# Additive attention: six of sixteen relus move to GpSimd, in pairs around its split

## The reference, cut to what matters

```
q = einsum('bnc,ac->bna', X, Wq);  k = einsum('bnc,ac->bna', X, Wk);  Vy = X @ Wy_w.T + Wy_b
e = relu(signed_sqrt(q[:, :, None, :] + k[:, None, :, :]))
scores = einsum('bija,a->bij', e, Wphi)
ex = exp(scores - max_j(scores));  denom = sum_j(ex)
Ew = einsum('bij,bija->bia', ex, e)
out = (einsum('bij,bjc->bic', ex, Vy) + Ew @ We_w.T + We_b * denom) / (denom + EPS_DEN)
```

## Time and profile before

| quantity | value |
|---|---|
| median of 3 runs | 6389.82 us (6387.81 to 6393.55) |
| profiled execution | 6392.27 us, span 6390.6 us |
| TensorE busy | 76% |
| VectorE busy | 72% |
| ScalarE busy | 63% |
| GpSimd busy | 24% |
| mean granted TensorE clock | 0.921 |

### The profile page before, as it was taken

The page is one execution under the profiler, slowest core; times in us unless marked ns, Lnnn a source line. Parts: engine busy times, 40 slices in busy tenths (PEclk is TensorE's granted clock), DMA queues, the critical chain, the costliest instruction groups (busy, mean ns, idle before and its releaser), DMA issues. The chain is left out here.

```text
span 6390.6 us, 74432 instructions
## 1 busy us (share of the span) xinstructions
PE 4886.3 (76%) x24108; PEld 2316.8 (36%) x24426; DVE 4620.4 (72%) x7027; ACT 4005.7 (63%) x2670; POOL 1540.2 (24%) x947
## 2 busy tenths in 40 slices
PE   5776867579964777777777777777777777749999
PEld 2332323357731222222222222222222222237777
DVE  2857658343335999999999999999999999942221
ACT  1011110210027999999999999999999999734443
POOL 1423424001001222222222222222222222213333
PEclk9988989789977999999999999999999999979999
DMA  1000000000011000000000000000000000020000
GB/s 74 0 0 0 0 0 0 31 3 10 10 67 38 2 3 2 3 2 13 3 2 3 2 15 2 2 3 2 3 9 4 2 2 4 3 79 14 13 13 7
DMA packets 37157, 70.97 MB, mean 11 GB/s; under 512 B 4576, under 2 KB 22080, under 8 KB 34240
## 3 DMA queue, kind: packets, MB, share of 16 engines
q1 hardware_dynamic: 34880, 62.53, 2.8%
q0 software_dynamic: 2176, 7.34, 0.3%
HBM read 49.94 MB, written 19.92 MB: 11 GB/s over the span
## 5 line engine op out<-in xcount | busy, mean ns | idle before, releaser
L732 DVE CUSTOM_DVE_ANT_0 e_slots<-e_slots,banks 128x1024 f32<-128x1024 f32 x2048 | 2418.6, 1216 | 219.5 <-PE banks L510 213.7
L572 ACT ACTIVATE e_slots<-e_slots,eps_rho 128x4096 f32<-128x4096 f32 x512 | 1885.7, 3707 | 17.7
L510 PE MATMUL banks<-ex_parts,sel 128*128 128x512 bf16 x3778 | 1216.6, 400 | 677.8 <-DVE ew L732 586.7
L467 PE MATMUL banks<-e_slots,w_score 128*32 128x512 f32 x8192 | 1158.6, 653 | 121.6 <-ACT e_slots L572 96.0
L563 ACT ACTIVATE e_slots<-k,qt 128x1024 f32<-128x1024 f32 x1024 | 1107.8, 1136 | 101.7 <-DVE ew L732 97.5
L510 PEld LDWEIGHTS banks<-ex_parts,sel 128*128 128x128 bf16 x4096 | 276.3, 100 | 1572.0 <-DVE ew L732 1329.0
L624 POOL TENSOR_SCALAR part<-ex,masks 128x1024 bf16<-128x1024 f32 x128 | 143.1, 1118 | 2745.5 <-ACT ex L579 1470.1
L689 DVE TENSOR_SCALAR e_slots<-k,qt 128x1024 f32<-128x1024 f32 x1024 | 753.3, 777 | 6.1 <-DVE den L703 6.0
L1546 PE MATMUL banks<-g_h,r_h 128*128 128x512 f32 x1024 | 410.4, 401 | 0.9 <-POOL g_l L1666 0.9
L476 PE MATMUL banks<-sel 128*128 128x256 bf16 x2304 | 406.2, 288 | 0.1
L1546 PE MATMUL banks<-g_l,r_h 128*128 128x512 f32 x1024 | 404.4, 395 | 0.0
(11 more groups left out here) (257 smaller groups left out, 6617.0 us busy)
## 6 DMA issues: line engine op xcount, KB each, us to landing
stage<-in_h SPq DMA_DIRECT2D x8, 1024.0 KB, 4.9
x_tokens<-in_x SPq DMA_DIRECT2D x1, 4096.0 KB, 17.8
w_down<-in_w_down SPq DMA_DIRECT2D x1, 4096.0 KB, 13.0
x_between<-x_tokens SPq DMA_DIRECT2D x8, 512.0 KB, 3.1
kx<-x_between SPq DMA_DIRECT2D x8, 512.0 KB, 4.7
v_all<-v_out POOLq DMA_DIRECT2D x8, 512.0 KB, 3.2
vy<-v_all SPq DMA_DIRECT2D x4, 1024.0 KB, 5.2
xg<-x_between SPq DMA_DIRECT2D x32, 128.0 KB, 2.5
```

Of the source, the lines that this page charges most:

```text
L467: ins = nc.tensor.matmul(banks[REP * COLG * g:REP * COLG * (g + 1), half, :], c_["w_score"][:, s, :], e_slots[:, par, COLG * s + g, half * ...
L510: ins = nc.tensor.matmul(spread[n % 2][:, half * W:(half + 1) * W], c_["sel"][:, n, :], ex_parts[:, par, half * W:(half + 1) * W], start=T ...
L572: nc.scalar.activation(e_slots[:, par, four, :], e_slots[:, par, four, :], ACT.Sqrt, bias=eps_rho[:, 0:1]).then_inc(sqrt_done, 1)
L732: nc.vector.tensor_tensor_reduce(out=e, in0=e, in1=spread[n % 2], scale=1.0, scalar=0.0, op0=ALU.mult, op1=ALU.add, accum_out=ew[:, q, pla ...
```

## The change

Z_BY becomes `PPPPAAAAAPPVVVVV`: GpSimd (P) makes the relus of places 0 to 3, 9 and 10, ScalarE those of 4 to 8, VectorE those of 11 to 15. GpSimd makes one as two instructions, max(min(k2, FLT_MAX), -q) and then (+ q) * 1.0, which is relu(k + q); it takes two places at a time (`two_z`), so that the second instruction of a place doesn't follow its first directly. Pairs (0, 1) and (2, 3) stand before the split of a tile, pair (9, 10) behind it. For this the queries are kept negated too (`q_pairs` and `qt` have one more dimension). The roots wait for a third semaphore, `z_p`, where places of GpSimd are among their four. ScalarE's list becomes: exponential, relus 5, 6, 7, table load, root 0, relu 8, roots 1, 2, 3, relu 4 of t+3, table load. VectorE makes relus 11 and 12 behind place 14, and 13, 14, 15 behind place 15. The group's end goes to places 2, 3, 14 and 15, behind the relus there. Scores are spread one piece per place, with m = 0 at place 15 of the tile before, and `keep_clock` has six places instead of eight.

```
-    Z_BY = "VVAAAAAAAAVVVVVV"
-    Z_AFTER = {1: [0], 2: [1], 14: [10, 11], 15: [12, 13, 14, 15]}
-    EXT_AT, MAX_AT, END_AT = 1, 6, 2
-    SCORES_AHEAD = {11: [0], 13: [1]}
-    SCORES_AT = {1: [2, 3], 2: [4], 3: [5], 4: [6], 5: [7]}
-    IDLE_AT, IDLE_PRODUCTS = (6, 7, 8, 9, 10, 12, 14, 15), 3
+    Z_BY = "PPPPAAAAAPPVVVVV"
+    Z_AFTER = {14: [11, 12], 15: [13, 14, 15]}
+    EXT_AT, MAX_AT, END_AT = 1, 6, {2: 0, 3: 1, 14: 2, 15: 3}
+    SCORES_AHEAD = {15: [0]}
+    SCORES_AT = {0: [1], 1: [2], 2: [3], 3: [4], 4: [5], 5: [6], 6: [7]}
+    IDLE_AT, IDLE_PRODUCTS = (8, 9, 10, 11, 12, 13), 3
+    FLT_MAX = 3.4028234663852886e38
...
# ScalarE
-            def first_root(t, par, freed):
-                for n in (2, 3):
-                    relu(t, par, n, freed)
-                sqrt(t, par, 0)
-            def other_roots(t, par, freed):
-                for n in (4, 5, 6, 7):
-                    relu(t, par, n, freed)
+            def before_exp(t, par, freed):
+                relu(t, par, 4, freed)
+            def behind_exp(t, par, freed):
+                for n in (5, 6, 7):
+                    relu(t, par, n, freed)
                 nc.scalar.preload_act_table(ACT.Sqrt)
-                sqrt(t, par, 1)
-                for n in (8, 9):
-                    relu(t, par, n, freed)
-                sqrt(t, par, 2)
-                sqrt(t, par, 3)
+                sqrt(t, par, 0)
+                relu(t, par, 8, freed)
+                for s in (1, 2, 3):
+                    sqrt(t, par, s)
...
# GpSimd
+            def two_z(t, par, two, freed):
+                count = Z_BY.count("P")
+                for i, n in enumerate(two):
+                    pool.wait_ge(qt_ready, t + 1)
+                    if freed is not None:
+                        pool.wait_ge(xb_freed, freed + (n + 3))
+                    pool.sem_inc(z_begun, 1)
+                    nc.gpsimd.tensor_scalar(e_slots[:, par, n, :], k2[:, :], FLT_MAX,
+                                            qt[:, par, 1, place(n):place(n) + 1], ALU.min, ALU.max).then_inc(z_clamped, 1)
+                for i, n in enumerate(two):
+                    e = e_slots[:, par, n, :]
+                    pool.wait_ge(z_clamped, t * count + z_count("P", n + 1))
+                    pool.sem_inc(z_begun, 1)
+                    nc.gpsimd.tensor_scalar(e, e, qt[:, par, 0, place(n):place(n) + 1], 1.0,
+                                            ALU.add, ALU.mult).then_inc(z_p, 1)
+            def step(t, par, last=False):
+                if not last:
+                    two_z(t + 2, par, (0, 1), t * NP)
+                    two_z(t + 2, par, (2, 3), t * NP)
+                pool.wait_ge(bc_done, t * NP)
+                parts(t + 1, 1 - par)
+                if not last:
+                    two_z(t + 2, par, (9, 10), t * NP)
...
# VectorE, at a new batch and in a tile
+                    dve.wait_ge(z_p, b * (NTI * Z_BY.count("P")))
-                nc.vector.tensor_copy(q_pairs[:, :], c_["q_next"][:, :]).then_inc(kq_taken, 1)
+                nc.vector.tensor_copy(q_pairs[:, 0, :], c_["q_next"][:, :])
+                nc.vector.tensor_scalar(q_pairs[:, 1, :], c_["q_next"][:, :], -1.0, None, ALU.mult).then_inc(kq_taken, 1)
-                    if ends is not None and END_AT <= n < END_AT + 4:
-                        group_end(ends, n - END_AT)
                     if queries is not None:
                         for m in Z_AFTER.get(n, ()):
                             z(t + 2, par, m, t * NP)
+                    if ends is not None and n in END_AT:
+                        group_end(ends, END_AT[n])
```

More of the change, by code:

```diff
@@ L195, in adaln_kernel @@
                      + LN_BUFFERS("k"))
-        c_ = phase([("e_slots", [P, 2, NP, T], fp32), ("k2", [P, T], fp32), ("q_pairs", [P, T // 2], fp32),
+        c_ = phase([("e_slots", [P, 2, NP, T], fp32), ("k2", [P, T], fp32), ("q_pairs", [P, 2, T // 2], fp32),
                     ("k2_next", [P, T], fp32), ("q_next", [P, T // 2], fp32), ("vy", [P, JT, C], fp32),
-                    ("xg", [P, CC, P], fp32), ("qt", [P, 2, NP], fp32), ("ex", [P, T], fp32),
+                    ("xg", [P, CC, P], fp32), ("qt", [P, 2, 2, NP], fp32), ("ex", [P, T], fp32),
                     ("part", [P, T], bf16), ("ex_parts", [P, 2, T], bf16), ("ex_t", [P, JT, GT, TI], fp32),
@@ L563, in relu @@
                 nc.scalar.activation(e_slots[:, par, n, :], k2[:, :], ACT.Relu,
-                                     bias=qt[:, par, place(n):place(n) + 1]).then_inc(z_a, 1)
+                                     bias=qt[:, par, 0, place(n):place(n) + 1]).then_inc(z_a, 1)
             def sqrt(t, par, s):
                 four = slice(COLG * s, COLG * (s + 1))
-                for who, sem_ in (("V", z_v), ("A", z_a)):
+                for who, sem_ in (("V", z_v), ("A", z_a), ("P", z_p)):
                     if who in Z_BY[four]:
@@ L632, in parts @@
                                         ALU.subtract).then_inc(parts_done, 1)
+            def two_z(t, par, two, freed):
+                count = Z_BY.count("P")
+                for i, n in enumerate(two):
+                    assert Z_BY[n] == "P"
+                    pool.wait_ge(qt_ready, t + 1)
[10 more added lines that the diff above has]
+                                            ALU.add, ALU.mult).then_inc(z_p, 1)
             pool.wait_ge(c_loaded, 16 * N_C_LOADS)
+            for par in range(2):
+                for two in ((0, 1), (2, 3), (9, 10)):
+                    two_z(par, par, two, None)
             parts(0, 0)
-            parts(1, 1)
-            with pool.Fori(1, TILES // 2) as u:
-                for par in range(2):
-                    pool.wait_ge(bc_done, u * (2 * NP) + (par - 1) * NP)
-                    parts(u * 2 + par, par)
+            def step(t, par, last=False):
[6 more added lines that the diff above has]
+                    two_z(t + 2, par, (9, 10), t * NP)
+            step(0, 0)
+            step(1, 1)
+            with pool.Fori(1, TILES // 2 - 1) as u:
+                step(u * 2, 0)
+                step(u * 2 + 1, 1)
+            step(TILES - 2, 0, True)
             end_phase(pool, ph["C"])
@@ L688, in z @@
                 dve.wait_ge(qt_ready, t + 1)
[L689 removed]
+                nc.vector.tensor_scalar(e_slots[:, par, n, :], k2[:, :], qt[:, par, 0, place(n):place(n) + 1], 0.0,
                                         ALU.add, ALU.max).then_inc(z_v, 1)
```

23 lines of the change are left out of this document (11 added, 12 removed).

## The result

| quantity | before | after |
|---|---|---|
| median (range) | 6388.8 us (6381.9 to 6393.6) | 6461.7 us (6458.1 to 6462.1) |
| ratio to before | | 1.0114, 95% interval 1.0096 to 1.0131 |
| span of the profiled execution | 6390.6 us | 6456.2 us |
| VectorE, ScalarE, GpSimd, TensorE busy | 72, 63, 24, 76% | 71, 55, 52, 75% |
| mean granted TensorE clock | 0.921 | 0.924 |

The change makes the kernel 73 us slower. The forecast was 6244 us, between 6130 and 6430; sign and range are both wrong.

A forecast was written before the change was run, and what follows sets the result against it. VectorE and ScalarE were taken to be at their limit, GpSimd idle for three quarters. Four tiles at 25.4 plus 5.2 us make 106.8 against 111.4, 146 us less over 127 tiles: 6244 us, range 6130 to 6430.

The forecast's parts named there:

- Prices of the new work: GpSimd's twelve new instructions per tile at 1.12 us each; with its split of 6.9 us, 20.1 us per tile.
- rival 2: GpSimd becomes the bound: 6360 us at 1.33 us an instruction, 7406 us at 2.14; chance 0.16.
- The collision: VectorE's five relus meet GpSimd's last pair and cost 2.25 us per tile, between 0.9 and 4.5.
- Turns: VectorE's relus and GpSimd's last pair alternate, relus waiting 0.25, 1.0 and 1.0 us: 2.25 us per tile; chance 0.50.
- rival 1: GpSimd keeps the port for its pair (6384 us) or VectorE for its burst (6250 to 6345); chance 0.24.
- rival 3: No collision worth naming, relus falling behind GpSimd's last pair; tiles of 24.8 us on ScalarE's loop, 6110 us; chance 0.10.
- ScalarE's wait: ScalarE waits 1.1 us per tile for the row maximum, making its loop 24.8 us.
- Small ones: Negated queries, added waits for GpSimd at the seam, six relus saved on ScalarE, TensorE's shifted scores and fillers: said to cancel.
- the clock: TensorE's shifted work cost nothing; a low clock in every tile would add 1.0 us per tile; chance 0.04.
- The group's end: VectorE's extra work per four tiles: 3.4 us plus 1.8 of meetings with GpSimd, 5.2 us, between 3.4 and 7.

The follow-up runs named there:

- e1: The kernel after with 52 satisfied waits ahead of phase C on VectorE, so its loop code lies 26 instructions later; 6337.7 us.
- e8: e1 with GpSimd's last pair (9, 10) 2 columns wide instead of 1024, so the output isn't the reference's; 6110.1 us.
- e9: e1 with six more idle TensorE products, whose result isn't used, at place 1; 6304.7 us.
- e4: The kernel before with only the group's end moved to places 2, 3, 14 and 15, where after has it; 6379.5 us.
- e11: e1 with the group's end back at places 2 to 5, as before the change; 6328.2 us.

## Why the prediction was wrong

**Prices of the new work: right.** GpSimd's instructions take 1.11 us free of a collision, as from the earlier trace rows; their means of 1176 and 1186 ns hold the meetings with VectorE. GpSimd isn't the bound (rival 2), and ScalarE waits for it ahead of a root only once, 6.9 us. (In rival 2 the 6360 us take in the group's end and the 7406 do not; nothing hangs on it.)

**The collision: right in kind, nearly in size.** Turns, 2.25 us forecast, 1.9 measured. Neither side goes through its burst while the other waits (rival 1). The shortest groups of e1 have their four tiles in 107 us (27.3, 25.9, 27.0 and 26.8), forecast 106.8. And rival 3's conditions, made real in e8, give 102.4 for four tiles and 6110 us; the prediction had 102.6 and 6110 for them. Part of this is luck. The shortest tile of e1 lasts 25.9 us, not 25.4, and what comes on top of four such is 3.4 us, not 5.2: misses of 2.0 and 1.8 us that cancel. For a kernel without falls and stops the sum was close: 127 tiles at 107.0 / 4 would be an estimated 154 us less than before's phase, forecast 146.

**ScalarE's wait: too small, and harmless.** 1.8 us a tile (224.8 / 124) for the maximum, 1.1 forecast. ScalarE isn't the bound, as it waits for VectorE's slots besides (418 us).

**"Small ones" is the step that failed,** with two terms.

The larger one isn't in the sum at all: the code. I counted instructions by their durations only, and took it for granted that an engine has its next instruction at hand. The profile of before held the sign, the row of stops ahead of the copy of the queries (4.4 us, 8 times) and 68 packets of instructions, and I passed over both. After had its loop 11 instructions earlier and 24 shorter, which put it over a block's border: 75 us of stops and, with the falls of the clock behind them (in 85 tiles instead of 53), 124 us in all (after against e1).

The other term is the clock, costed at nothing because TensorE "waits for VectorE before most spreads", with "+1.0 us per tile" as a risk that took 0.04 of the chance. At places 3 to 6 it is the other way round: there a piece of the scores stands ahead of each spread, and VectorE waits for TensorE, 0.6 us in a tile at full clock and 2.1 with a fall. The falls were there before the change and cost plain tiles nothing; now a tile with one mostly lasts 1.5 to 2.0 us longer. In e1 the splits go from 2006.9 to 5489.6 us: 27.42 us per tile, 0.55 less than before and not 1.15, where tiles without falls would give 1.2. That is why the shifted kernel gains 53 us (by the profiled executions 65) and not 146. The scores did double, as written (1.06 to 1.94 us), but the wait is VectorE's for the spreads behind them and not ScalarE's for the maximum, 1.7 us in either stretch. What makes one group fall and its neighbour not, I can't say; e9 shows only that work for TensorE at place 1 wins 33 us of it back.

**The group's end** was costed at 5.2 us, a collision of its parts at 1.8 of them; the tiles show 3.4. e4 and e11 show no more than 0.3% for its place in either direction; that part of the change neither helps nor explains the loss.

## What to carry to other kernels

Before a difference of 1 or 2% is put down to an edit of a long unrolled loop, look for idle time named "issue" at the loop's head and for packets on the instruction queue, and run a control in which only the code is moved by some satisfied waits. Price the work of an engine that takes turns with another by where in the tile it lies: six relus a tile on GpSimd are worth 53 us with the last pair beside VectorE's relus and 229 us with all pairs beside its reductions. And ask of each longer stretch of one engine what TensorE does in it: its clock is paid for in the tiles behind, once the engine that waits for it has lost its slack.

## What the runs showed of the hardware that was new to me

- A loop on VectorE of 281 or 305 instructions is fetched anew in each pass or not, by its place alone; the engine then stands still 0.3 to 3.7 us per pass in the mean, until 1.7 to 2.3 us after a packet of code starts. Moving the kernel before by 118 instructions costs 71 us (6390 to 6462); its stops are 56 us, against 4 at the old place.
- Fetches come in packets of 8.2 KB; the places of all kernels agree with three blocks of 128 instructions that stay and a fourth that doesn't.
- VectorE's relus and GpSimd's one-input instructions take turns, one by one: 2.52 us for two relus and 2.64 for GpSimd's two at the same time, 1.41 to 1.44 and 2.22 to 2.25 alone. Neither starves.
- In the kernel after TensorE's granted clock was at 0.50 ahead of VectorE's two stops, through them, and for 4.0 us after TensorE's next product (4005.6 to 4009.6).
- The same fall of TensorE's clock is free or not by who sets the pace: nothing in a plain tile of the kernel before, 1.5 to 2.0 us in a tile of e1.
